# Layer 0 of a scan tower: the order of fetches, placings and weight splits in its opening

## What is computed

```python
x = embedding[tokens] + pos_enc[:S][None]
for l in range(4):
    h = layernorm(x, g, bt)                  # gain and bias are folded into the weights by the kernel
    uv = h @ Wi.T + bi;  u, v = uv[..., :D], uv[..., D:]
    uc = dwconv_causal(u, cw, cb)            # 4 taps along the sequence
    delta = softplus(uc @ wd.T + bd); Bm = uc @ wB.T + bB; Cm = uc @ wC.T + bC
    # h = h * exp(-delta) + uc * Bm, y = sum(h * Cm): exp(-softplus(z)) is sigmoid(-z)
    y = selective_scan(uc, delta, Bm, Cm) * sigmoid(v)
    x = x + (y @ wo.T + bo)
x = x + attention(layernorm(x));  x = x + int8_ffn(layernorm(x))
```

## Time and profile before

| | before |
|---|---|
| device time, median of 3 runs | 1655.63 us (1651.02 to 1657.86) |
| profiled execution | 1659.81 us |
| its span | 1657.9 us, 36360 instructions, mean granted TensorE clock 0.966 |
| TensorE, matmul | 1555.3 us busy (94%) |
| VectorE | 1365.5 us (82%) |
| ScalarE | 1238.9 us (75%) |
| GpSimd | 747.5 us (45%) |

### The profile page before, as it was taken

The page is one execution under the profiler, slowest core; times in us unless marked ns, Lnnn a source line. Parts: engine busy times, 40 slices in busy tenths (PEclk is TensorE's granted clock), DMA queues, the critical chain, the costliest instruction groups (busy, mean ns, idle before and its releaser), DMA issues.

```text
span 1657.9 us, 36360 instructions
## 1 busy us (share of the span) xinstructions
PE 1555.3 (94%) x11137; PEld 1229.3 (74%) x11137; DVE 1365.5 (82%) x3414; ACT 1238.9 (75%) x2875; POOL 747.5 (45%) x1354
## 2 busy tenths in 40 slices
PE   3699999999999999999999988999999999999985
PEld 2578788878888888888888875666666666666653
DVE  4699999889999899999999875678888878888864
ACT  2587788688888778888888844677777777777763
POOL 6656633223333233333333244555565555555542
PEclk9799999999999999999999995999999999999997
DMA  7121100000000000000000000000000000000000
GB/s 165 31 59 28 23 8 1 1 33 0 0 1 1 1 1 0 0 1 1 1 0 0 1 1 1 2 7 11 11 10 15 10 10 10 10 10 10 15 12 25
DMA packets 16397, 21.98 MB, mean 13 GB/s; under 512 B 2928, under 2 KB 13808, under 8 KB 16304
## 3 DMA queue, kind: packets, MB, share of 16 engines
q1 hardware_dynamic: 13232, 14.54, 2.7%
q0 software_dynamic: 3072, 6.30, 2.4%
HBM read 14.14 MB, written 6.29 MB: 12 GB/s over the span
## 4 chain that ended last, share of the span: by engine, by line
PE 62%; ACT 14%; DVE 12%; issue 9%; POOL 1%; DMA 1%; DVEq 1%; ACTq 0%; POOLq 0%
PE bank L595 9%; PE bank L586 7%; PE bank L775 5%; PE bank L732 4%; PE bank L746 4%; PE bank L718 4%; PE bank L759 4%; PE bank L711 3%; PE bank L721 3%; PE bank L712 3%; PE bank L676 3%; ACT xs L1028 2%; DVE x L1360 2%; ACT ht L1018 2%; PE bank L606 2%
## 5 line engine op out<-in xcount | busy, mean ns | idle before, releaser
L1071 ACT ACTIVATE probs<-bank 128x512 f32<-128x512 f32 x384 | 207.1, 591 | 133.8 <-PE bank L759 131.0
L1406 DVE TENSOR_REDUCE mx<-bank 128x2 f32<-128x512 f32 x384 | 246.1, 682 | 26.6 <-PE bank L746 25.0
L441 POOL TENSOR_TENSOR x<-x,bo_row 128x768 f32<-128x768 f32 (+1 forms) x64 | 118.9, 1858 | 188.0 <-DVE ucr_r L1305 188.0
L586 PE MATMUL bank<-ht,w_uv 128*128 128x512 f32 x576 | 171.0, 407 | 16.5 <-ACT sv_l L1051 11.5
L759 PE MATMUL bank<-q_t,k_t 64*128 64x256 f32 x768 | 157.2, 353 | 8.7 <-ACT probs L1071 5.5
L417 POOL TENSOR_TENSOR lnt<-mv,const 128x4 f32<-128x4 f32 x64 | 20.5, 321 | 311.9 <-DVE mv L1270 311.8
L746 PE MATMUL bank<-k_t,q_t 64*128 64x256 f32 x768 | 141.2, 325 | 6.2 <-ACT k_t L1082 3.1
L1296 DVE SCALAR_TENSOR_TENSOR uc_h<-u_h,vec,uc_h 128x512 f32<-128x512 f32 x192 | 143.9, 750 | 2.9 <-ACT uc_h L989 2.9
L586 PEld LDWEIGHTS bank<-ht,w_uv 128*128 128x128 f32 x576 | 111.2, 196 | 46.3 <-issue 16.6
L1279 DVE SCALAR_TENSOR_TENSOR xs<-x,rstd,xs 128x192 fp32r<-128x192 f32 x256 | 90.0, 413 | 59.4 <-ACT xs L1028 59.4
L759 PEld LDWEIGHTS bank<-q_t,k_t 64*128 64x128 f32 x768 | 103.0, 188 | 39.7 <-issue 21.3
(11 more groups left out here) (178 smaller groups left out, 4668.9 us busy)
## 6 DMA issues: line engine op xcount, KB each, us to landing
out_dram<-y_out SPq DMA_DIRECT2D x32, 192.0 KB, 2.0
raw_z<-w_z_dram SPq DMA_DIRECT2D x4, 704.0 KB, 5.3
raw_uv<-w_uv_dram SPq DMA_DIRECT2D x4, 576.0 KB, 3.9
emb<-embedding_dram,idx POOLq DMA_INDIRECT x64, 3.6
q_t<-mx_t SPq DMA_DIRECT2D x64, 6.0 KB
w_o<-w_o_dram SPq DMA_DIRECT2D x1, 768.0 KB, 5.4
bo_row<-bout_dram SPq DMA_DIRECT2D x4, 96.0 KB, 6.6
w_qkv<-w_qkv_dram SPq DMA_DIRECT2D x1, 288.0 KB, 7.1
```

The costliest lines, as they stand in the source:

```text
L441: nc.gpsimd.tensor_tensor(rows, rows, bo_row[:, l, :][:, None, :].broadcast_to([P, CT, D]), ALU.add).then_inc(x_biased, 1)
L586: last = nc.tensor.matmul(out[:], w, r[:], start=(k == 0), stop=(k == len(passes) - 1))
L1071: last = act.activation(probs[:, (s + g // 2) % 2, g % 2, 2 * j * S:2 * (j + 1) * S], B_ST[j][:], ACT.Exp, scale=float(DH) ** -0.5)
L1406: last = nc.vector.tensor_reduce(mx[:, s, :, j * H // 2 + g], B_S[j][:].rearrange("p (t k) -> p t k", t=2), AX, ALU.max)
```

## The change

In words: GpSimd's constants are set ahead of the first fetch; only the fetches of items 0 and 1 precede the first deviation, item 2's follows it, and item 3's comes in step 0. In each step GpSimd now runs deviation, fetch, bias, index instead of index, fetch, deviation, bias. VectorE places an item's rows at the end of its step instead of the start; item 1's statistics and variance and item 0's rest are taken into the prologue, ahead of the split of the weights; the centring comes ahead of place(1). The rests of U and V are formed ahead of those of z, and TensorE waits for two of the four before `uv` and for all four before `z_c`. ScalarE runs one small sigmoid first.

```diff
@@ setup
+        table = sb("table", [P, 1])
@@ GpSimd, prologue
             for n in range(FIRST):
                 index(n, n, n % 2)
-            for n in range(FIRST):
+            for k, value in enumerate((EPS, -0.5, 1.5)):
+                nc.gpsimd.memset(const[:, k, :], value).then_inc(s_zero, 1)
+            for n in range(2):
                 wait(pool, s_idx4, n + 1)
                 gather(n, n, n % 2)
-                if n == 1:
-                    for k, value in enumerate((EPS, -0.5, 1.5)):
-                        nc.gpsimd.memset(const[:, k, :], value).then_inc(s_zero, 1)
-                    pool.wait_ge(s_zero, 3)
...
+            pool.wait_ge(s_zero, 3)
             inverse_deviation(item(0))
+            wait(pool, s_idx4, 3)
+            gather(2, 2, 0)
 
             def step(at, l, k):
-
-                for lag, stage in ((-4, index), (-3, gather)):
-                    it = at(lag)
-                    if it is not None and it[1] == 0 and (l > 0 or k is None or k - lag >= FIRST):
-                        stage(it[0], it[2], it[3])
+                fetched, indexed = at(-3), at(-4)
+                if fetched is not None and fetched[1] == 0:
+                    wait(pool, s_idx4, fetched[0] + 1)
                 inverse_deviation(at(-1))
+                if fetched is not None and fetched[1] == 0:
+                    gather(fetched[0], fetched[2], fetched[3])
                 bias_rows(at(0))
+                if indexed is not None and indexed[1] == 0:
+                    index(indexed[0], indexed[2], indexed[3])
@@ TensorE, uv
                 if first_of_layer(it):
-                    pe.wait_ge(w_split, 4 * (l + 1))
+                    pe.wait_ge(w_split, 4 * l + 2)
@@ TensorE, z_c
+                if first_of_layer(it):
+                    pe.wait_ge(w_split, 4 * (l + 1))
@@ ScalarE
             act.wait_ge(s_ident, 2)
+            act.activation(table[:], ident[:, 0:1], ACT.Sigmoid)
             act.activation(identr[:], ident[:], ACT.Identity).then_inc(s_identr, 1)
@@ VectorE, split_weights
                 for k in range(2):
-                    nc.vector.tensor_tensor(w_z_rest[:, s, k, :], raw_z[:, k, :], w_z[:, s, k, :].bitcast(F32),
+                    nc.vector.tensor_tensor(w_uv_rest[:, s, k, :], raw_uv[:, k, :], w_uv[:, s, k, :].bitcast(F32),
                                             ALU.subtract).then_inc(w_split, 1)
                 for k in range(2):
-                    nc.vector.tensor_tensor(w_uv_rest[:, s, k, :], raw_uv[:, k, :], w_uv[:, s, k, :].bitcast(F32),
+                    nc.vector.tensor_tensor(w_z_rest[:, s, k, :], raw_z[:, k, :], w_z[:, s, k, :].bitcast(F32),
                                             ALU.subtract).then_inc(w_split, 1)
@@ VectorE, prologue
             variance(item(0))
+            centre_weights(0)
             place(1, 1, 1)
-            centre_weights(0)
+            rows_there(item(1))
+            statistics(item(1))
+            statistics_there(item(1))
+            variance(item(1))
+            rest_of_rows(item(0))
             split_weights(0)
@@ VectorE, step
-                it = at(-2)
-                if it is not None and it[1] == 0:
-                    place(it[0], it[2], it[3])
-                rows_there(at(-1))
+                opening = l == 0 and k == 0
+                if not opening:
+                    rows_there(at(-1))
                 recurrence(at(4))
-                statistics(at(-1))
-                statistics_there(at(-1))
+                if not opening:
+                    statistics(at(-1))
+                    statistics_there(at(-1))
...
-                variance(at(-1))
+                if not opening:
+                    variance(at(-1))
                 other_taps(at(2), (1, 2))
-                rest_of_rows(at(0))
+                if not opening:
+                    rest_of_rows(at(0))
                 save_y(at(4))
                 rest_of_uc(at(2), 1)
                 rest_of_uc(at(2), 0)
                 residual(at(4))
+                it = at(-2)
+                if it is not None and it[1] == 0:
+                    place(it[0], it[2], it[3])
```

## The result

| | before | after |
|---|---|---|
| device time, median of 18 runs each | 1652.76 us (1650.99 to 1661.10) | 1664.72 us (1654.88 to 1669.61) |
| ratio, 95% interval | | 1.0063 [1.0049, 1.0076] |
| profiled execution, its span | 1659.81, 1657.9 us | 1669.61, 1667.7 us |
| mean granted TensorE clock | 0.966 | 0.952 |
| inp_h of item 0 starts | 78.77 us | 72.10 us |

The change costs 0.6%, some 10 us (the medians differ by 12.0), where 3.5 us less were forecast. The last two rows, from the time order of VectorE, say where: item 0 is 6.7 us early, item 10 is 9.3 us late, and that lag hardly changes up to the end of the span (9.8 us). So the opening gains, and ten steps of layer 0 lose 16.0 us.

What follows compares the result with a forecast made beforehand. The opening was bound by waits on GpSimd's fetches, landing rows and the table load, not TensorE; layer 0's steps had placing on VectorE's path. 5.1 - 1.6 = 3.5 us less than 1655.6 gave 1652, eight-in-ten range 1643.5 to 1659.

Steps and rivals of the forecast that it cites:

- Part 1: Opening on GpSimd: item 0's deviation starts at 16.6 us, and uv(0) at 26.7, 10.3 us earlier.
- Part 2: Opening, next delay: item 3's rows land and are placed at 40.1 us, leaving a gain of 5.3 us, not 10.3.
- Part 3: VectorE's placing directly ahead of the statistics: its own wait adds 0.12 us each, taken as 0.15 in the loop.
- Part 4: ScalarE's table load moves to its first instruction: 1.3 us gained at uv(1).
- Part 5: Opening summed at uv(1): start at 49.5 us, a gain of 5.1 us, bounds 3.6 and 8.
- Part 6: Steps of layer 0: cheaper placings but bias holding VectorE 0.45 us a step; a loss of 1.6 us, 7.0 with full hold.
- Part 7: Later layers: swapping the order of the weight rests changes nothing.
- rival C: Layer 0 steps: bias takes the scans first, 1.8 us of hold in nine steps, 7.0 us lost; 1657.5 us, chance 0.13.

Runs made afterwards that it cites:

- g1_table_alone: The kernel before with one edit, the sigmoid's table loaded at the start by one small ScalarE activation: 1657.09 us, ratio 1.0001 to before.
- e5_opening_alone: The changed kernel's opening, and from step 4 on the steps of the kernel before: 1651.6 us, ratio 0.9961 to before.
- f3_small_bias: The changed kernel with layer 0's output bias added on one column of each tile instead of 192: 1648.31 us, ratio 0.9957 to before.
- f5_filler_half: The changed kernel with 16 repeated transposes ahead of TensorE's wait for hc_h in steps 6 to 15 of layer 0: 1662.67 us, ratio 1.0044 to before.
- f4_late_hc: The kernel before with three unused scans added ahead of hs_h in steps 6 to 15 of layer 0: 1672.91 us, ratio 1.0089 to before.
- f2_place_in_wait: e1_fetch_first with the placing moved, from step 4 of layer 0, ahead of the rest of the rows: 1643.1 us, ratio 0.9905 to before.
- e1_fetch_first: The changed kernel with GpSimd's fetch ahead of the deviation from step 4 of layer 0, placing still at step's end: 1654.74 us, ratio 0.9982 to before.

## Why the prediction was wrong, step by step

- **Part 1** (deviation at 16.6, uv(0) at 26.7): right, 16.28 and 26.40.
- **Part 2** (rows of item 3 placed at 40.1): 40.41, right in part by luck: the last fetch was issued at 32.94, 1.0 us later than forecast, and its rows were there 7.5 us on, not 8.2. That bias(0) and place(2) don't meet was wrong: they met at 33.26, and place(2) took 2.3 us more. It was hidden by the wait for item 3's rows.
- **Part 3** (0.12 to 0.15 us for a placing's own wait): right. A placing free of the bias was to take 0.87 + 0.15 = 1.02 us from VectorE; in after it is issued at 157.10 and inp_h starts at 158.08, 0.98 (1.16 at 172.35).
- **Part 4** (table, 1.3 us): the load is gone from the opening; 2.0 us earlier at item 0 in `g1_table_alone`. On the time it is not resolved.
- **Part 5** (uv(1) at 49.5, a gain of 5.1, bounds 3.6 to 8): 48.10, a gain of 6.5. At item 0 it was 6.7, at item 1 5.0 (89.87 against 94.91). The one miss is bias(1): forecast from 43.4, among the taps, it ran from 47.28, behind them, since deviation(2) began only at 38.26 (its variance stood behind the held place(2)) and the four fetch issues ran from 41.86 to 47.26. `e5_opening_alone` shows 6.4 us in the time, with an interval of 4.1 to 8.9.
- **Part 6** (a loss of 1.6, at worst 7.0): the step of the prediction that failed. It lost 16.0 us in the trace, and some 13 to 17 in the time (1.0063 less the opening's 0.9961 makes 17 us; the fetch's place alone 13). Its frame held: a step free of holds was to be 15.19 - 1.57 + 1.02 = 14.64 us, and is 14.69 in after and 14.7 in `f3_small_bias`. The placings on the path were counted right as well. The rest, a hold of 0.45 us a step, failed in three ways.
  1. **Where the bias falls was off by 1.6 us.** From V, the end of the variance (149.88 in the step from item 4), inp_h starts at V + 8.20 (158.08), the bias at V + 9.02 (158.90), and the first scan is issued at V + 9.26 (159.14). So the bias is 0.8 us behind inp_h and ahead of both scans; it was put 2.4 behind, when both scans hs_h are over. The bias itself came 0.9 earlier than the forecast V + 9.9: nothing held the fetch up, and no gap stood between its end and the bias. And inp_h came 0.7 later: 2.4 behind means V + 7.5, while the prediction's own place at V + 7.1 with 1.02 for it makes V + 8.1. That slip of the sum was enough by itself to put the bias, at V + 9.9, into the second scan. In the two steps in which VectorE was late at its xs (2.46 us of waiting at 136.40), place was issued at 140.75 and 206.55, within 0.25 us of the bias (140.50 and 206.73), and was held in the scans' stead. The prediction said against rival C that a held VectorE would move the bias out of the scans; three steps in a row (159.14, 174.57, 191.46) show that it doesn't; in `f5_filler_half` it moves on to hs_l in four steps (157.05 is the first), which is held for as long.
  2. **The hold was sized too small.** Pairs of scans took 0.84 to 1.98 us more than 1.26, and the two placings 1.48 and 1.90 more: 11.9 us in all, where the sum had nine times 0.45, 4.1. Hidden under the wait for xs is only a part of it: the step from item 5, with 1.49 us of hold and a full clock, took 15.43 against 14.69, so 0.7 us. By `f5_filler_half` against `f3_small_bias`, 13.5 us of hold cost at most 8.2; in that proportion the 11.9 would cost some 7 (an estimate), which is what rival C had.
  3. **TensorE's clock was left out of the steps.** It was given 3 us either way, taken from the slice of the opening, with no path by which the change would move it. The chain hc_h late, TensorE idle, clock at 0.50, TensorE on the path wasn't among the rivals, though rows 1 and 6 showed the clock at its lower level beside idle stretches of TensorE. `f4_late_hc` makes it without any hold, `f5_filler_half` has the holds without it; between item 2 and item 10 it is 9.5 us of the loss in the profiled execution.
- **Part 7** (later layers, nothing): the lag of after is 9.3 us at item 10, 10.1 at item 63 and 9.8 at the end; nothing above the scatter is to be seen. No run took the swap of the rests by itself, so it is argued, not shown.

The Trainium skill (SBUF — State Buffer, SBUF: two separate sides) calls the pair of ports an exclusive lock that is kept for the whole instruction, with the loser blocked. The prediction set this beside its own softer sum. Holds of 0.84 to 1.58 us beside a bias of 1.85 agree with the Trainium skill. Those of 1.90 (206.55), 1.98 (174.57) and 2.33 us (33.26) are longer than the bias beside them: there VectorE's operation was issued ahead of the bias, while a fetch was still being issued, and waited for the bias all the same. A lock that is kept for one instruction doesn't account for these by itself. By the Trainium skill alone the loss of rival C, 7.0 us, would have been the forecast for this part, still short by the clock.

Which of the chances was right: rival C named the holds and their place, with 0.13, and its hold of 1.8 us is near what was seen, but it had nothing of the clock; slower by over 0.5% had 0.07. What remains open: why the granted clock fell after an idle time of 1.46 us at 213.04 and not after 1.49 at 163.17, or, in before, after 1.53 at 116.17, while the same 1.53 at 109.67 in `e5_opening_alone` stood beside a fall of 13.7 us. The traces show the falls; they don't show what decides. The first of after's three falls may thus not be due to the held scan alone.

## What to carry to other kernels

Before an operation is moved on GpSimd, list what stands beside its new place on VectorE with two SBUF inputs, over the whole spread of the step and not at one offset, and price each meeting at the full length of the operation. Then follow what is held to TensorE: a wait of 1.5 to 3 us there can cost a second time through the clock, 3.1 us for a fall of 13.7, and most of it shows in the step behind. And put an operation that must be done somewhere where its engine waits in any case: moving the placing there made 0.8% (`f2_place_in_wait` against `e1_fetch_first`).

## What the runs showed of the hardware beyond the forecast

- An operation of VectorE can be held for longer than the GpSimd operation beside it lasts. The place at 33.26 took 3.29 us instead of 0.96 with a bias of 1.81: it also stood still through the end of a fetch's issue. The pair of scans at 174.57 took 3.24 instead of 1.26 with a bias of 1.84 that began 0.83 us behind it (175.40), and the scan at 157.05 of `f5_filler_half` 2.68 instead of 0.66.
- Scans are held as much as additions are: 2.10 to 3.24 us a pair in after, 1.26 in `f3_small_bias`.
- It works the other way too: the issue of an indirect fetch took 4.19 us instead of 0.95 (103.65), while VectorE made the weight rests and began the recurrence; another 2.53 at 23.66. In `f5_filler_half` the same meeting went against VectorE: the issue took 1.64, and the rests of U and V 3.20 instead of 1.03.
- Idle times of TensorE of 1.5 to 3.1 us went, in some cases, with a granted clock of 0.50 for 10.2 to 13.7 us (111.6, 179.9, 214.0 in after), and in other cases with none; in `f4_late_hc` waits of 2.13 to 3.27 us with 3.4 to 13.7 us of it.
- Repeated transposes ahead of the wait kept the clock at 1.00 from 118 to 230 us in both runs that had them, with scans held as in after.
